# Edge stage of a two-layer graph network: order of the layers, sums and stores within a step

## What is computed

```python
a   = mlp((x[src] + x[dst]) * 0.5)      # 3 hidden layers of 64 with relu, an output layer, a layer norm over 64
flux = 0.5 * (flux_send + flux_recv) - 0.5 * a * (x[src] - x[dst])
agg  = segment_sum(flux, dst, 12500)
x    = layernorm(x + (x + agg))
```

## Time and profile before

| what | value |
|---|---|
| median of 3 runs | 11443.35 us |
| time of the profiled execution | 11389.55 us |
| its span, first to last instruction | 11387.5 us |
| busy: PE / PEld / DVE / ACT / POOL | 65% / 51% / 31% / 26% / 45% |
| granted TensorE clock, mean | 0.755 |
| DMA, mean | 101 GB/s |

### The profile page before, as it was taken

How to read it: one execution, slowest core, us unless ns; L and a number is a source line. 1 busy time by engine, 2 the same in 40 slices (tenths; PEclk the granted TensorE clock), 3 DMA queues, 4 the chain that set the end, 5 groups by cost and what they waited for, 6 DMA issues and landing times. The chain is left out here.

```text
span 11387.5 us, 219939 instructions
## 1 busy us (share of the span) xinstructions
PE 7417.4 (65%) x80448; PEld 5752.3 (51%) x80850; DVE 3539.5 (31%) x7714; ACT 3006.3 (26%) x5496; POOL 5117.5 (45%) x5109
## 2 busy tenths in 40 slices
PE   2788887766767676566666666566666666666665
PEld 1688886655656565444444444444444444444443
DVE  5777772111122222222222222222222222222222
ACT  0677772000000000122222222222222222222222
POOL 3555553444333333444444444444444444444443
PEclk6899998777877777676777777777777777777777
DMA  3333334333433333333333333333333333333332
GB/s 103 114 115 116 115 115 149 127 125 118 139 106 121 109 122 109 98 84 85 88 89 87 87 87 90 89 90 90 90 87 88 89 88 89 90 91 87 95 89 72
DMA packets 641238, 1145.18 MB, mean 101 GB/s; under 512 B 396177, under 2 KB 449533, under 8 KB 622971
## 3 DMA queue, kind: packets, MB, share of 16 engines
q0 software_dynamic: 214272, 516.37, 18.5%
q1 hardware_dynamic: 410670, 584.51, 15.5%
q10 hardware_dynamic: 15197, 28.99, 0.9%
HBM read 924.17 MB, written 205.22 MB: 99 GB/s over the span
## 5 line engine op out<-in xcount | busy, mean ns | idle before, releaser
L1765 POOL DMA_INDIRECT edge_rows<-node_table,edge_et x3224 | 3097.2, 961 | 3535.4 <-DMA edge_et<-edges_turned 2402.2
L1290 PE MATMUL two_acc<-x_parts,two_win 128*128 128x192 bf16 x16072 | 1738.4, 270 | 522.9 <-issue 503.3
L1290 PEld LDWEIGHTS two_acc<-x_parts,two_win 128*128 128x128 fp8e4 x16072 | 1530.2, 108 | 692.1 <-issue 655.8
L815 POOL DMA_INDIRECT two_rows<-x_parts,src_at x1120 | 1056.8, 944 | 1802.6 <-PE two_edge_acc L1076 1352.5
L1816 PE MATMUL edge_seg<-edge_rows,edge_sel 128*32 128x66 f32 x6448 | 1076.6, 260 | 361.6 <-issue 349.8
L1820 PE MATMUL edge_seg<-edge_rows,edge_sel 128*32 128x66 f32 x6448 | 1093.8, 262 | 306.2 <-issue 305.7
L1818 PE MATMUL edge_seg<-edge_z,edge_sel_r 128*32 128x66 f32 x6448 | 997.9, 267 | 338.6 <-issue 336.9
L1817 PE MATMUL edge_seg<-edge_rows,edge_sel 128*32 128x66 f32 x6448 | 1009.2, 266 | 290.7 <-issue 289.4
L1819 PE MATMUL edge_seg<-edge_zx,edge_sel_r 128*32 128x66 f32 x6448 | 977.4, 268 | 326.9 <-issue 325.7
L1048 ACT ACTIVATE one_win<-one_count 128x784 fp8e4<-128x784 f32 x1312 | 1066.8, 824 | 379.4 <-PE one_count L999 240.9
L1966 DVE RECIPROCAL edge_ssq<-edge_ssq 128x8 f32<-128x8 f32 x403 | 81.8, 203 | 3468.5 <-ACT edge_ssq L1874 3129.0
(11 more groups left out here) (327 smaller groups left out, 11220.5 us busy)
## 6 DMA issues: line engine op xcount, KB each, us to landing
two_win<-adjacency SPq DMA_DIRECT2D x82, 3136.0 KB
adjacency<-one_win SPq DMA_DIRECT2D x41, 3136.0 KB
edge_near<-near_ids SPq DMA_DIRECT2D x403, 192.0 KB
edge_rows<-node_table,edge_et POOLq DMA_INDIRECT x3224
node_sums<-edge_seg SPq DMA_DIRECT2D x806, 33.0 KB
two_rows<-x_parts,src_at POOLq DMA_INDIRECT x1120
edge_yd<-y_parts SPq DMA_DIRECT2D x806, 12.0 KB
node_table<-two_row SPq DMA_DIRECT2D x49, 260.0 KB
```

Source lines behind the costliest of these rows:

```text
L815: pool.indirect_dma_start(rows[:, b % 2, e, :], None, XP.rearrange("p (j c) -> (p j) c", c=3 * C), bass.IndirectOffsetOnAxis(ap=src_at[:, ...
L1290: mm = pe.matmul(acc[b][:, half * 3 * C:(half + 1) * 3 * C], win[:, b, half, j, :].bitcast(FP8), now[:, j, :], start=(j == 0), stop=(j == ...
L1765: pool.indirect_dma_start(rows[:, h.b, t, :], None, T5, bass.IndirectOffsetOnAxis(ap=et[:, h.b, 0, t:t + 1].bitcast(I32), axis=0))\
```

## The change

All of a chunk's layers are done in its own step on TensorE, with `sums` of h - 2 between `turn` and `layer` 1. ScalarE does `take_y` of h, `squares` of h - 1, the first `relu` of h, `take` of h - 2, `root` of h - 1, then the other two `relu` of h. VectorE's `scale` is one chunk back, stores are six back. No operation is added or removed; the last steps after the loop are fewer. Below, the first lines are the head of `edge_pass`, the next `step` is TensorE's, the last one ScalarE's.

```diff
-    LAG = 5
-    BACK = 8
+    LAG = 1
+    BACK = 6
...
             def step(h):
-                turn(h)
                 for k, run in stages:
                     if not early(h, k):
                         run(h.back(k))
 
-            stages = ((1, lambda h: layer(h, 1)), (2, lambda h: layer(h, 2)), (3, last), (4, sums))
+            stages = ((0, turn), (2, sums), (0, lambda h: layer(h, 1)), (0, lambda h: layer(h, 2)), (0, last))
             chunks(pe, step, HS, RB)
-            for c in range(HS, HS + 4):
-                for k, run in stages:
-                    if c - k < HS:
-                        run(Chunk(0, c - k, RB))
+            for c in range(HS - 2, HS):
+                sums(Chunk(0, c, RB))
...
             def step(h):
-                take_y(h)
                 for k, run in stages:
                     if not early(h, k):
                         run(h.back(k))
...
-            stages = ((1, lambda h: relu(h, 0)), (2, lambda h: relu(h, 1)), (3, lambda h: relu(h, 2)), (4, squares), (5, take), (4, root))
+            stages = ((0, take_y), (1, squares), (0, lambda h: relu(h, 0)), (2, take), (1, root), (0, lambda h: relu(h, 1)), (0, lambda h: relu(h, 2)))
             chunks(act, step, HS, RB, DONE_LAG)
-            for c in range(HS, HS + 5):
+            for c in range(HS, HS + 2):
                 for k, run in stages:
                     if c - k < HS:
                         run(Chunk(0, c - k, RB))
```

## The result

The changed kernel took 12062.3 us, median of three runs (12027.62 to 12067.47), against 11443.35: a ratio of 1.055 [1.0515, 1.0585], or +619 us. That is slower, as forecast, but 2.3 us above the upper end of the range and far above the +250 of the sum.

A forecast was written before the change was run, and what follows sets the result against it. The edge stage is bound by a loop of ScalarE's copy, `et` and gather, with TensorE's time behind the gather; 253 + 10 - 13 = +250 us gives 11640, or 11690 on the median's level; range 11400 to 12060.

The forecast's parts named there:

- The sign and its mechanism: SyncE's turn 7: slower, as `done_made` comes later; waits of about 25 us or more instead of 12.5; chance 0.55.
- The round: Eight edge steps around SyncE's wait for `done_made`: 137.5 us, 5.5 more per round taken, times 46 = 253 us.
- three steps without a gather: TensorE during SyncE's long wait: copies of three steps follow at about 8 us each, where 6 before.
- The catch-up: Gathers after SyncE's wait: successors at SyncE's own pace of 11.3 us; then two ordinary steps of 17.0.
- The clock: TensorE's layers in gather-free steps: at granted clock 0.50, 5.8 us per round, 266 us at most; taken at nothing.
- The relus' gaps: TensorE's waits before `layer` 2 and `last`: 0.8 us each, 1.6 per step without gathers; no cost beside a gather.
- The ordinary step: Edge steps with a gather: +0.3 us each from more instructions beside the gather, near 17; 10 us over 35 steps.
- The end: Stores after the loop: 12 left instead of 16 at 3.1 us each, -13 us.
- Every wait on the path: Rival, TensorE's step: both relu waits stretch every step by 1.6 us, 645 us, 12090, up to 12350; chance 0.13.
- Unchanged: Rival, edge stage: copy, `et` and gather set the step in both kernels, 11443 +- 50; chance 0.12.
- Faster: Rival, gaps between close gathers: TensorE gets a second step done, -470 us, 10970, or half, 11200; chance 0.20.
- The picture of one delivery queue: TensorE beside a gather: what it has done is delivered through one queue, in order, at some 5 per us.

The follow-up runs named there:

- experiments 1 and 2: 1: store of `out` moved from SyncE to ScalarE: after 0.9958, before 0.9995. 2: before with SyncE stop added 1.0486; after with `done` ahead of `scale` 1.0058.
- experiment 4: Slow chip, before 11265.36 us: new order with longer SyncE stop 12095.25, before with shorter inserted stop 11301.05, new order without any stop 11572.13.

## Why the prediction was right or wrong

**The sign and its mechanism: right.** VectorE's turn 6 now comes two TensorE steps later, and SyncE's wait grows. I said 25 us or more instead of 12.5; it was 31.2. That this wait is a cause, and not only a sign, is shown by the two by two of experiments 1 and 2 on the quick chips (before 7365, before with it 7722, after 7720; after without it 7332, on a chip where before takes 7363), and on a slow chip by the 523 us between the new order with a longer stop and without one.

**The round: right in shape, too small in size. This is the step that failed.** The forecast had 137.5 us for eight steps and took 5.5 more than before, which puts before at 132.0; that is what the 46 rounds took, 132.1. After, they took 146.1: 14.0 more, 642 of the 672 us between the spans. (The 35 steps ahead of them add 44, where +10 was forecast; the start and the end take 14 off.) Between ScalarE's copies of half u = 0, by which the forecast counted, the 44 whole rounds between the first and the last have these means:

| part of the round | forecast, us | measured, us |
|---|---|---|
| the ordinary step ahead of the stop | 17.0 | 17.1 |
| three steps without a gather | 24.0 | 27.1 (10.9, 8.1, 8.1) |
| two steps of catch-up | 62.5 | 59.2 (35.0, 24.3) |
| two steps behind it, taken as ordinary | 34.0 | 43.0 (24.0, 19.0) |
| sum | 137.5 | 146.5 |

Two terms were sized wrong:
- *The catch-up*, 5.8 of the 9.0 us. It doesn't end after two steps. I had the next gathers "at SyncE's own pace, 11.3 us", four of its steps in 45.2; behind the stops of 45 rounds they took 53.7 on the mean (50.4 to 58.7), so the two steps behind are not ordinary yet. In the round above they took 54.4, and in the step of 20.7 SyncE stood in no wait for another engine: its own instructions came slower (`yd` in 7.07 instead of 1.53) while GpSimd issued gathers without a gap, from 6291 to 6321 us. I had priced SyncE from one row of a round with looser gathers.
- *The clock*, 2.7 us, taken at nothing: next paragraph.

**The clock: wrong to take nothing.** In the last two of the three steps the granted clock is 1.00, that is 2.4 GHz, and each takes 8.1 us. The first begins in the slow phase that the gather leaves, at 0.50, that is 1.2 GHz (0.50 from 7275 to 7285 us; the earlier trace rows have the same right after a gather). Windows from copy to copy: this first step in one round, the step behind it, and the first step of another round:

```profile
7274.48:7287.69 13.21, 11.25 (x135) 7.75 (x128) 4.79 (x14) 4.45 (x10) 0.00 (x0) 0.53 0.00 1
7287.69:7295.83 8.14, 6.36 (x132) 4.63 (x125) 3.47 (x9) 4.53 (x11) 0.00 (x0) 1.00 0.01 2
7133.24:7143.08 9.84, 8.05 (x134) 5.53 (x126) 4.79 (x14) 4.34 (x10) 0.00 (x0) 0.82 0.00 0
```

In 17 of 44 rounds that step has a mean clock of 0.54 and takes 13.0 us, and from the last gather ahead of the stop to the next such gather the round takes 149.3; in the other 27 it has 0.83 and takes 9.7, and the round takes 145.0. So this time reaches the round, as far as such means can show it; no run changes the clock alone. On the mean the low clock costs 10.9 - 8.1 = 2.7 us per round, 126 us in all, about half of the 266 of the upper end. What decides between 0.54 and 0.83, the runs don't show.

The relus' gaps are another matter. In the two steps at 1.00 TensorE waits 0.8 to 1.0 for each `relu`, which I had at 0.8, and the clock stays up:

```profile
7290.37 1.12 PE L1793 MATMUL edge_mp<-edge_h,edge_W 128*128 128x512 f32 x2 [0.78 <-ACT edge_h L1856]
7292.50 1.05 PE L1803 MATMUL edge_zp<-edge_WO,edge_h 128*128 128x128 f32 x8 [1.01 <-ACT edge_h L1856]
```

The Trainium skill's rule on idleness (TensorE: Matmul & The Clock Gate, part 1), read so that any added gap counts, would have the sum at its upper end; gaps of 1 us did not bring the clock down from 1.00 here.

**The ordinary step: right.** 17.0 was forecast, 0.3 above the 16.7 of before. Ahead of the rounds the steps take 409.7 / 24 = 17.1, and before 401.2 / 24 = 16.7.

**The end: right.** 12 stores in 37.84 us, were 16 in 49.97: -12.1, forecast -13.

```profile
11989.35 37.84 SPq L1713 DMA_DIRECT2D node_sums<-edge_seg  x12
```

**The rivals.** "Every wait on the path" had 645 us and comes nearest to the number, by another way: it needs 1.6 us more in every step, and where neither order stops the step grew by 0.35 to 0.38 on the slow chips. All relu waits are kept in the new order without the stop, and that was 0.4% faster than before on the quick chips and lost 2.7% on the slow one. "Unchanged" is out with rounds of 146.1 for 132.1. "Faster" needed gaps of about 2.5 us between the close gathers, in which TensorE does a second step; there are such gaps (10.81 us ahead of the gather at 6332.26), but they come from SyncE being late, so no time is won:

```profile
6332.26 0.94 POOL L1765 DMA_INDIRECT edge_rows<-node_table,edge_et  x1 [10.81 <-DMA edge_et<-edges_turned]
```

**The picture of one delivery queue** for what TensorE has done gave the ordinary step of 17.0, and the even steps of experiment 4 have its loop. It wasn't tested by itself, and it doesn't cover all that the trace shows: SyncE's own issues come slower too beside gathers without a gap, so a cause common to both engines (how their instructions arrive, for one) is a rival that no run here separates.

## What to carry to other kernels

When an engine's jobs are brought nearer to each other, look for the wait of a third engine that a late job now holds: here a store that nobody was in need of stood in the queue that also starts the gathers, and a wait there is paid in gathers. Put such a wait on an engine with slack, or ahead of what makes it late (two exchanged calls in VectorE gave back 309 of 355 us on a quick chip). And price the catch-up behind a long wait from rows in which the same queues are as full as they will be then, not from the ordinary step; and look at the granted clock of each step in it, not of one.

## What was not expected of the hardware

The same program takes 7363 us on one chip and 11265 or 11443 on another. The window of the kernel before in a quick chip's stage, beside gathers without a gap, then the eight last matmuls of half u = 1 there and the copy that waited for them:

```profile
5200.00:5210.00 10.00, 7.22 (x121) 5.30 (x120) 3.87 (x11) 4.01 (x9) 7.70 (x8) 0.84 0.57 137
```

```profile
5207.89 0.40 PE L1825 MATMUL edge_seg<-edge_seg,edge_edge_now 128*1 128x66 f32 x8 [2.73 <-ACT edge_seg L1882]
...
5208.44 0.23 ACT L1882 ACTIVATE edge_seg<-edge_seg 128x66 f32<-128x66 f32 x1 [0.60 <-PE edge_seg L1825]
```

TensorE starts 241 instructions in these 10 us, 24 per us, where the chip of the forecast starts 5.3 beside a gather, and ScalarE's copy starts 5208.44 - 5208.29 = 0.15 us behind the matmuls' end, where on that chip it started 5 us behind the earlier trace rows. The Trainium skill (Perfetto Trace Analysis, Tensor Engine Instruction) says that a matmul's end in a profile is a model and that its semaphore is pushed only after PSUM acknowledges; that allows for a distance between the two, and these rows give its size on either chip, not its cause. Why two chips do this and the others don't, no run here shows. The slow kind makes another engine the bound (TensorE and the loop through it, not GpSimd's issue), so the same edit is worth 0.9958 on one and 1.027 on the other: a version that beats both kernels on the quick chips, the new order with that store on ScalarE (0.9958), loses to before on the slow one.
